# A three-stage decoder layer on one core: reordering the prologue in front of the batch loop

## The chip, the cores and the metric

The kernel runs on one core of a Trainium2 chip. The time is device microseconds (us) of one execution. Five engines work from queues of their own, each strictly in its written order: PE (TensorE), DVE (VectorE), ACT (ScalarE), POOL (GpSimd) and SP (SyncE), which here only issues DMAs. They meet through semaphores.

## The reference

For each of 8 batches of 256 tokens with 512 features:

```
i, f, g = x @ Wi.T, x @ Wf.T, x @ Wg.T
a = sigmoid(f);  b = silu(i) * (1 - a)
h[t] = a[t] * h[t-1] + b[t]                      # scan over tokens
xg = h * silu(g)
y = xg * rsqrt(mean(xg^2) + 1e-5) * w_norm
x1 = layernorm(x + y @ Wo.T)
x2 = layernorm(x1 + wkv(w, u, k=x1, v=ctx))      # exponential weights, a scan over tokens
w1q, w2q = per-row int8 quantise-dequantise of w_gate_up (2816x512), w_down (512x1408)
gate, up = quantised(x2) @ w1q.T
out = layernorm(x2 + quantised(silu(gate) * up) @ w2q.T)
```

## The kernel before, in words

A batch passes through three stages. Stage 1 is `project(b, k)`: six half projections (k = 0, 1 forget, 2, 3 input, 4, 5 gate), each 24 matmuls because every fp32 operand is split into a high and a low part (`split_half`, `split_x`: high part on ACT, low part on DVE or POOL). ACT reads each half (`read_projection`), DVE does `weigh_inputs`, `recurrence`, `gating`, ACT and DVE split the result (`split_states`), PE multiplies it by Wo (`project_out(b, t)`, one of two blocks of 128 tokens) and sums its squares (`sum_squares`), then `mean_square`, `rms_scale`, `residual_1`, `layer_norm_1`, `rstd_1` and `normalise_1` give x1. Stage 2 turns x1 (`turn_keys`), takes exponentials and scans (`sum_weights`, `denominator`, `sum_values`, `numerator`, `divide`, `refine`), turns the result back (`turn_values`) and normalises it (`residual_2`, `layer_norm_2`, `rstd_2`, `normalise_2`, `scale_2`). Stage 3 is the quantised MLP (`turn_inputs`, `mlp_up`, `scale_products`, `silu`, `hidden`, `hidden_max_row`, `mlp_down`). All three run at once on three neighbouring batches in a loop; in front of the loop a prologue fills this pipeline, written out call by call for each engine. The diff touches only the prologue (lines 438 to 476 of SP, 724 to 797 of PE, 1062 to 1150 of ACT, 1374 to 1405 of POOL, 1786 to 1850 of DVE).

The prologue also prepares the MLP weights, in 15 loads q = 0 to 14 ("rows"), of which 0 to 10 hold two blocks of w_gate_up (512 KB) and 11 to 14 one block of w_down (704 KB). A load passes through five engines: `load_rows` (SP), `weigh_rows` (DVE: row maximum, scale, inverse), `round_rows` (POOL), `turn_rows` (PE, 8 or 11 transposes), `keep_rows` (ACT). Loads 0 to 10 share three buffers of the ring, so load q waits until load q - 3 has been turned:

```
elif q >= RING:
    sp.wait_ge(rows_turned, last + 1)
```

`last` is 3 for q = 6, 4 for q = 7 and 5 for q = 8. The scales of the rows also go out to HBM and back: `turn_scales(0)` (PE), `read_scales(0)` (ACT), `store_scales(0)` (SP, waits for the former), `spread_scales(0)`. SP's list has `store_scales(0)` between loads 7 and 8.

`exp_tables` and `silu_tables` switch ACT's function table. `warm_up` and `keep_busy(n)` are transposes of the identity whose output is not used; `keep_busy` stands where PE would have nothing to do.

## Time and profile before

| | |
|---|---|
| median of 3 runs | 418.21 us (418.01 to 418.85) |
| profiled execution | 415.5 us, span of its instructions 413.7 us |
| PE busy | 90% of the span |
| DVE, ACT, POOL busy | 88%, 77%, 54% |
| mean granted TensorE clock | 0.978 |

The median lies 2.7 us above the profiled execution. All durations below are of that one profiled execution, so a sum is made against its span and carried over to the median as a difference.

Up to about 130 us the prologue runs, then the loop, with PE busy nearly all the time, and from about 345 us the last batches. The slices of the page show the prologue as the part with digits below 9 on PE. Work that arrives later at the loop moves all that follows.

### The profile page before, as it was taken

How to read it: one execution, taken by the hardware profiler on the slowest of the kernel's cores; microseconds unless marked ns; L12 is line 12 of the kernel's file. 1: busy time of each engine (PE TensorE's matmuls, PEld its weight loads, DVE VectorE, ACT ScalarE, POOL GpSimd, SP SyncE). 2: the span in 40 equal slices, each digit the busy share in tenths (PEclk: the TensorE clock that was granted, in tenths of full speed). 3: DMA queues.
4: the chain of work that ended last, by engine and by line, in shares of the span. 5: the costliest groups of instructions: out<-in, count | busy, mean ns of one | idle time of the engine just before them, and what ended most of it. 6: DMA issues, size and time to landing. Idle time of an engine off the chain costs nothing.

```text
span 413.7 us, 7886 instructions
## 1 busy us (share of the span) xinstructions
PE 370.7 (90%) x2756; PEld 290.6 (70%) x2778; DVE 362.6 (88%) x620; ACT 320.0 (77%) x422; POOL 223.8 (54%) x274
## 2 busy tenths in 40 slices
PE   7798899989898899999999999999999999386862
PEld 7797798769775778678776977697759774133331
DVE  3889899869767999999998999899989998997684
ACT  3688599597928989599959995999599967975671
POOL 1674564833435726674667546654676454745451
PEclk9999999999999999999999999999999999688997
DMA  7978356011200013000400040005000300000101
GB/s 255 370 259 325 102 194 242 0 52 27 103 1 2 0 58 122 2 26 27 153 1 27 3 177 2 25 0 177 0 25 0 128 0 25 25 1 2 51 27 52
DMA packets 12843, 31.75 MB, mean 77 GB/s; under 512 B 2038, under 2 KB 5132, under 8 KB 12812
## 3 DMA queue, kind: packets, MB, share of 16 engines
q1 hardware_dynamic: 12812, 31.35, 21.7%
q8 instruction: 18, 0.29, 0.3%
q14 instruction: 13, 0.11, 0.1%
HBM read 27.14 MB, written 4.21 MB: 76 GB/s over the span
## 4 chain that ended last, share of the span: by engine, by line
PE 50%; DVE 15%; ACT 13%; issue 10%; POOL 8%; DMA 2%; SPq 1%; POOLq 0%; DVEq 0%; ACTq 0%
PE proj_ps L506 29%; PE slot_ps L611 10%; PE slot_ps L646 5%; POOL ring L1300 2%; DMA ring<-w_gate_up_dram 2%; ACT L1013 2%; DVE hid_top L1654 2%; PE proj_ps L691 1%; DVE stats L1590 1%; PE slot_ps L631 1%; ACT xqT L955 1%; DVE num L1583 1%; DVE ring L1635 1%; ACT L1017 1%; ACT turn_ps L918 1%
## 5 line engine op out<-in xcount | busy, mean ns | idle before, releaser
L611 PE MATMUL slot_ps<-w1q,xqT 128*128 128x512 bf16 (+1 forms) x377 | 80.1, 362 | 5.7 <-ACT xqT L955 2.9
L1300 POOL TENSOR_TENSOR ring<-ring 128x512 f32<-128x512 f32 (+1 forms) x48 | 61.3, 1284 | 36.0 <-ACT ring L964 36.0
L611 PEld LDWEIGHTS slot_ps<-w1q,xqT 128*128 128x128 bf16 x384 | 35.9, 98 | 44.8 <-issue 3.5
L506 PE MATMUL proj_ps<-x_high,proj_high 128*128 128x256 f32 x384 | 64.8, 290 | 0.8 <-ACT proj_high L891 0.4
L506 PE MATMUL proj_ps<-x_low,proj_high 128*128 128x256 f32 x384 | 61.5, 282 | 0.0
L506 PE MATMUL proj_ps<-x_high,proj_low 128*128 128x256 f32 x384 | 61.5, 282 | 0.0
L506 PEld LDWEIGHTS proj_ps<-x_high,proj_high 128*128 128x128 f32 x384 | 53.1, 189 | 2.8 <-issue 0.7
L506 PEld LDWEIGHTS proj_ps<-x_high,proj_low 128*128 128x128 f32 x384 | 52.7, 188 | 0.0
L506 PEld LDWEIGHTS proj_ps<-x_low,proj_high 128*128 128x128 f32 x384 | 52.6, 188 | 0.0
L1275 POOL TENSOR_TENSOR den<-den,q_state 128x512 f32<-128x512 f32 x16 | 27.5, 1736 | 38.0 <-ACT q_state L924 38.0
L646 PE MATMUL slot_ps<-w2q,hqT 128*128 128x512 bf16 x161 | 42.1, 405 | 6.6 <-ACT hqT L978 5.8
L964 ACT ACTIVATE ring<-ring,zero_bias,x_scale 128x512 f32<-128x512 f32 (+1 forms) x48 | 36.8, 771 | 10.4 <-DVE ring L1635 10.3
L971 ACT ACTIVATE ring<-ring,round_bias,hid_inv 128x768 f32<-128x768 f32 (+1 forms) x32 | 29.6, 966 | 10.4 <-DVE hid_inv L1676 10.4
L1635 DVE TENSOR_TENSOR ring<-slot_ps,scale_rows 128x512 f32<-128x512 f32 (+1 forms) x48 | 30.6, 638 | 6.8 <-PE slot_ps L611 6.4
L646 PEld LDWEIGHTS slot_ps<-w2q,hqT 128*128 128x128 bf16 x176 | 16.6, 103 | 25.9 <-issue 8.9
L1236 POOL TENSOR_SCALAR ring<-ring,row_inv 128x512 f32<-128x512 f32 (+1 forms) x24 | 25.3, 1068 | 17.4 <-DVE row_inv L1730 17.4
L1552 DVE TENSOR_TENSOR_SCAN p_state<-decay_col,num 128x256 f32<-128x256 f32 x32 | 31.7, 1049 | 0.0
L1638 DVE TENSOR_TENSOR ring<-slot_ps,scale_rows 128x512 f32<-128x512 f32 (+1 forms) x48 | 30.5, 636 | 0.0
L1654 DVE TENSOR_REDUCE hid_top<-ring 128x1 f32<-128x1408 f32 x15 | 24.1, 1609 | 4.5 <-POOL ring L1300 4.5
L1270 POOL TENSOR_TENSOR num<-num,c_sb 128x512 f32<-128x512 f32 x16 | 20.5, 1286 | 13.7 <-ACT num L908 13.4
L978 ACT ACTIVATE hqT<-slot_ps,half_bias 128x768 bf16<-128x768 f16 (+1 forms) x32 | 25.3, 836 | 3.2 <-PE slot_ps L631 3.1
L1017 ACT ACT_TABLE_LOAD x18 | 23.1, 1283 | 1.0 <-PEq L1986 0.7
(146 smaller groups left out, 809.8 us busy)
## 6 DMA issues: line engine op xcount, KB each, us to landing
ring<-w_gate_up_dram SPq DMA_DIRECT2D x11, 512.0 KB, 4.3
forget<-xT_dram SPq DMA_DIRECT2D x8, 512.0 KB, 3.6
x_sb<-x_dram SPq DMA_DIRECT2D x8, 512.0 KB, 3.6
c_sb<-cT_dram SPq DMA_DIRECT2D x8, 512.0 KB, 4.4
out_dram<-late SPq DMA_DIRECT2D x16, 256.0 KB, 2.1
late<-w_down_dram SPq DMA_DIRECT2D x2, 704.0 KB, 6.6
ring<-w_down_dram SPq DMA_DIRECT2D x2, 704.0 KB, 4.2
scale_rows<-scratch_dram SPq DMA_DIRECT2D x2, 704.0 KB, 5.9
```

The costliest lines, as they stand in the source:

```text
L506: last = nc.tensor.matmul(out, a, b, start=(i == 0), stop=(i == len(terms) - 1))
L611: last = nc.tensor.matmul(slot_ps[:, s, half * 512:half * 512 + width], xqT[:, par, d, t * P:(t + 1) * P], w1q[:, d, half * I + at:half * ...
L646: last = nc.tensor.matmul(slot_ps[:, s, 0:D], hqT[:, i, :], w2q[:, i, :], start=(i == 0), stop=(i == IB - 1))
L964: nc.scalar.activation(g, g, ACT.Silu, bias=zero_bias[:, :], scale=x2_scale[:, par, t:t + 1]).then_inc(silu_ready, 1)
L971: nc.scalar.activation(h, h, ACT.Identity, bias=round_bias[:, :], scale=hid_inv[:, t:t + 1]).then_inc(hid_rounded, 1)
L1017: nc.scalar.preload_act_table_set("silu_and_others")
L1275: nc.gpsimd.tensor_tensor(blocks(den, h), blocks(den, h), blocks(rec_copy, h), ALU.mult).then_inc(newton_ready, 1)
L1300: nc.gpsimd.tensor_tensor(hid, hid, gate_buf[:, at:at + width], ALU.mult).then_inc(hid_ready, 1)
L1552: last = nc.vector.tensor_tensor_scan(p_state[:, c, 1:], decay_col[:, c:c + 1].to_broadcast([P, T]), num[:, c, :], 0.0, ALU.mult, ALU.add)
L1635: nc.vector.tensor_tensor(gate_buf[:, at:at + width], slot_ps[:, s, 0:width], scale_rows[:, at:at + width], ALU.mult).then_inc(gate_scaled, 1)
L1638: nc.vector.tensor_tensor(hid_buf(t)[:, at:at + width], slot_ps[:, s, 512:512 + width], scale_rows[:, I + at:I + at + width], ALU.mult).th ...
L1654: nc.vector.tensor_reduce(hid_top[:, :], hid_buf(t)[:, 0:I], AX.X, ALU.max, apply_absolute_value=True).then_inc(hid_top_ready, 1)
```

## The change

SP issues the halves of the projection weights ahead of the rows. PE does three projections before the first `turn_rows`, each of the others before one; `turn_rows(3)` stands in front of `project_out(0, 0)`, and 4 and 5, the scales, 6 and 7 stand together behind `project_out(0, 1)`. DVE's `gating(0)` and `biases` come earlier among the `weigh_rows`, `weigh_rows(7)` comes after `layer_norm_1(0)`, and `residual_2(0)`, `layer_norm_2(0)` come ahead of `weigh_rows(12)`, `normalise_2` and `scale_2` ahead of `weigh_rows(13)`. ACT and POOL follow. PE's filler transposes shrink: 80 to 64 at the start, 56 to 28 before `project_out(0, 0)`, 92 to 32 before `turn_values(1, 0)`.

```diff
@@ SP
             load_half((0, 0))
             load_xT(0)
-            load_rows(0)
             load_half((0, 1))
             load_columns()
             load_half((1, 0))
+            load_rows(0)
+            load_half((1, 1))
+            load_half((2, 0))
             load_rows(1)
-            load_half((1, 1))
+            load_half((2, 1))
             load_rows(2)
-            load_half((2, 0))
-            load_half((2, 1))
+            load_half((OUT_PROJ, 0))
+            load_half((OUT_PROJ, 1))
             load_rows(3)
             load_x(0)
             load_rows(4)
-            load_half((OUT_PROJ, 0))
             load_rows(5)
-            load_half((OUT_PROJ, 1))
             load_rows(11)
@@ PE
-                for _ in range(40):
+                for _ in range(32):
...
             project(0, 0)
+            project(0, 1)
+            project(0, 2)
             turn_rows(0)
-            project(0, 1)
+            project(0, 3)
             turn_rows(1)
-            project(0, 2)
+            project(0, 4)
             turn_rows(2)
-            project(0, 3)
-            project(0, 4)
             project(0, 5)
-            for q in range(3, 6):
-                turn_rows(q)
-            turn_scales(0)
             keep_busy(28)
-            pe.wait_ge(xg_ready, 1)
-            keep_busy(28)
+            turn_rows(3)
             project_out(0, 0)
             sum_squares(0)
             project_out(0, 1)
+            turn_rows(4)
+            turn_rows(5)
+            turn_scales(0)
             turn_rows(6)
             turn_rows(7)
             keep_busy(16)
...
             project_out(1, 0)
             sum_squares(1)
+            project_out(1, 1)
             turn_rows(12)
-            project_out(1, 1)
...
             project(2, 5)
-            pe.wait_ge(proj_read, 2 * PROJ + 5)
-            keep_busy(28, proj_ps[:, 0, 0:P // 2])
-            pe.wait_ge(num_ready, 4)
-            keep_busy(36, proj_ps[:, 0, 0:P // 2])
-            pe.wait_ge(h_ready, 3)
-            keep_busy(28, proj_ps[:, 0, 0:P // 2])
+            pe.wait_ge(mlp_read, 3)
+            keep_busy(32)
             turn_values(1, 0)
@@ ACT
             read_projection(0, 1)
+            split_half((2, 1))
+            forget_gate(0)
+            read_projection(0, 2)
+            split_half((OUT_PROJ, 0))
             keep_rows(0)
-            forget_gate(0)
-            split_half((2, 1))
+            split_half((OUT_PROJ, 1))
+            read_projection(0, 3)
             keep_rows(1)
-            read_projection(0, 2)
-            read_projection(0, 3)
-            split_half((OUT_PROJ, 0))
+            read_projection(0, 4)
             keep_rows(2)
-            split_half((OUT_PROJ, 1))
-            read_projection(0, 4)
             read_projection(0, 5)
-            keep_rows(3)
-            read_scales(0)
             split_states(0)
             square(0)
             split_x(1)
+            keep_rows(3)
             keep_rows(4)
             exp_tables()
             decay()
-            for q in range(5, 7):
-                keep_rows(q)
+            keep_rows(5)
+            read_scales(0)
+            keep_rows(6)
...
-            keep_rows(12)
             round_2(0, 0, 0)
             round_2(0, 0, 1)
+            keep_rows(12)
@@ POOL
-            for q in range(6):
+            for q in range(4):
                 round_rows(q)
             pair_squares(0)
+            round_rows(4)
             split_x(1)
+            round_rows(5)
+            rms_scale(0)
             round_rows(6)
-            rms_scale(0)
             round_rows(7)
             rstd_1(0)
...
+            pair_squares(1)
+            rstd_2(0)
+            split_x(2)
             round_rows(12)
-            pair_squares(1)
-            split_x(2)
-            rstd_2(0)
@@ DVE
             split_first_x()
+            split_half((0, 1))
+            split_half((1, 0))
             weigh_rows(0)
-            split_half((0, 1))
+            split_half((1, 1))
+            split_half((2, 0))
             weigh_rows(1)
-            split_half((1, 0))
-            split_half((1, 1))
+            split_half((2, 1))
             weigh_rows(2)
-            split_half((2, 0))
+            split_half((OUT_PROJ, 0))
+            weigh_inputs(0)
+            recurrence(0)
+            split_half((OUT_PROJ, 1))
+            biases()
             weigh_rows(3)
-            split_half((2, 1))
+            gating(0)
             weigh_rows(4)
-            weigh_inputs(0)
+            split_states(0)
             weigh_rows(5)
-            recurrence(0)
-            split_half((OUT_PROJ, 0))
-            gating(0)
-            split_half((OUT_PROJ, 1))
-            split_states(0)
-            biases()
-            for q in range(6, 8):
-                weigh_rows(q)
             mean_square(0)
+            weigh_rows(6)
             residual_1(0, 0)
             residual_1(0, 1)
             layer_norm_1(0)
+            weigh_rows(7)
             weigh_rows(8)
...
             gating(1)
-            weigh_rows(12)
-            split_states(1)
             residual_2(0, 0)
             residual_2(0, 1)
+            split_states(1)
             layer_norm_2(0)
+            weigh_rows(12)
+            normalise_2(0, 0)
+            mean_square(1)
+            scale_2(0, 0)
             weigh_rows(13)
-            mean_square(1)
-            normalise_2(0, 0)
             residual_1(1, 0)
-            scale_2(0, 0)
             residual_1(1, 1)
```

On PE from the end of `project(0, 5)` to the start of `project(1, 0)`, before (L506 with proj_high is `project`, with wo_high `project_out`; L665 is `turn_rows`, L678 `turn_scales`, L691 `keep_busy`, L540 `sum_squares`):

```order
L506 MATMUL proj_ps<-x_low,proj_high 128x256 x4
L665 MATMUL slot_ps<-identity,ring 128x128 x24
L678 MATMUL slot_ps<-identity,row_scale 11x128
L691 MATMUL slot_ps<-identity 128x128 x56
L506 MATMUL proj_ps<-wo_high,xg_high 128x512 x4
...
L506 MATMUL proj_ps<-wo_low,xg_high 128x512 x4
L665 MATMUL slot_ps<-identity,ring 128x128 x16
L691 MATMUL slot_ps<-identity 128x128 x16
L506 MATMUL proj_ps<-x_high,proj_high 128x256 x4
```

and the same stretch now:

```order
L691 MATMUL slot_ps<-identity 128x128 x28
L665 MATMUL slot_ps<-identity,ring 128x128 x8
L506 MATMUL proj_ps<-wo_high,xg_high 128x512 x4
...
L506 MATMUL proj_ps<-wo_low,xg_high 128x512 x4
L665 MATMUL slot_ps<-identity,ring 128x128 x16
L678 MATMUL slot_ps<-identity,row_scale 11x128
L665 MATMUL slot_ps<-identity,ring 128x128 x16
L691 MATMUL slot_ps<-identity 128x128 x16
L506 MATMUL proj_ps<-x_high,proj_high 128x256 x4
```

Transposes of rows 4 and 5 moved from ahead of the two `project_out` to behind them.

On DVE from `mean_square(0)` (msq) over `residual_1` and `layer_norm_1` (stats, mv) to the next rows, before:

```order
L1724 TENSOR_REDUCE row_max<-ring 128x2
L1727 TENSOR_SCALAR row_scale<-row_max 128x2
L1730 RECIPROCAL row_inv<-row_scale 128x2
L1504 TENSOR_SCALAR msq<-turn_ps 128x2
L1512 SCALAR_TENSOR_TENSOR inp<-proj_ps,rms,x_sb 128x512 x2
L1520 BN_STATS stats<-inp 128x6 x2
L1524 BN_AGGR mv<-stats 128x2 x2
L1724 TENSOR_REDUCE row_max<-ring 128x2
```

and now (three lines lower in number for the same functions):

```order
L1501 TENSOR_SCALAR msq<-turn_ps 128x2
L1721 TENSOR_REDUCE row_max<-ring 128x2
L1724 TENSOR_SCALAR row_scale<-row_max 128x2
L1727 RECIPROCAL row_inv<-row_scale 128x2
L1509 SCALAR_TENSOR_TENSOR inp<-proj_ps,rms,x_sb 128x512 x2
L1517 BN_STATS stats<-inp 128x6 x2
L1521 BN_AGGR mv<-stats 128x2 x2
L1721 TENSOR_REDUCE row_max<-ring 128x2
```

Before, the row maxima ahead of msq were of loads 6 and 7 and the one behind mv of load 8; now load 6 stands behind msq, and the one behind mv is of load 7.

On POOL in front of the first norm's `rstd_1(0)` (ve, neg_mean), now; L1231 is `round_rows`, two instructions to a load, L1244 `rms_scale(0)`:

```order
L1231 TENSOR_SCALAR ring<-ring,row_inv 128x512 x2
L1244 TENSOR_TENSOR rms<-msq,minus_half 128x2
L1231 TENSOR_SCALAR ring<-ring,row_inv 128x512 x4
L1250 TENSOR_TENSOR ve<-mv,eps_col 128x2
```

Loads 6 and 7 are both rounded between `rms_scale(0)` and `rstd_1(0)`; before, load 6 came ahead of `rms_scale(0)`.

## Rows read from the trace of the kernel before

**Rows 1.** The page: span, engines, and the granted clock in 40 slices.

```profile
span 413.7 us, 7886 instructions
PE 370.7 (90%) x2756; PEld 290.6 (70%) x2778; DVE 362.6 (88%) x620; ACT 320.0 (77%) x422; POOL 223.8 (54%) x274
PEclk9999999999999999999999999999999999688997
```

**Rows 2.** Timeline, PE, 36 to 47 us: start, us, line, tile, count [idle before].

```profile
36.89 1.16 PE L506 MATMUL proj_ps<-wo_high,xg_high 128*128 128x512 f32 x4 [0.48 <-DVE xg_low L1498]
43.47 0.62 PE L665 MATMUL slot_ps<-identity,ring 128*128 128x128 f16 x8
46.97 0.71 PE L506 MATMUL proj_ps<-x_high,proj_high 128*128 128x256 f32 x4
```

**Rows 3.** Timeline, DVE, 25 to 70 us, the same columns.

```profile
25.70 1.31 DVE L1479 SCALAR_TENSOR_TENSOR inp<-forget,inp 128x1024 f32<-128x1024 f32 x1 [0.55 <-ACT inp L859]
26.93 1.21 DVE L1724 TENSOR_REDUCE row_max<-ring 128x2 f32<-128x1024 f32 x1
28.60 2.29 DVE L1487 TENSOR_TENSOR_SCAN inp<-forget,inp 128x1024 f32<-128x1024 f32 x1
35.42 1.21 DVE L1498 TENSOR_TENSOR xg_low<-inp,xg_high 128x1024 fp32r<-128x1024 f32 x1
36.55 1.25 DVE L1735 TENSOR_SCALAR u_cap<-u_col 128x4 f32<-128x4 f32 x1
37.91 2.25 DVE L1740 TENSOR_SCALAR key_bias<-key_bias 128x4 f32<-128x4 f32 x1
51.91 1.60 DVE L1724 TENSOR_REDUCE row_max<-late 128x1 f32<-128x1408 f32 x1
53.84 1.26 DVE L1534 TENSOR_TENSOR_SCAN q_state<-decay_col,turn_ps 128x256 f32<-128x256 f32 x2
69.36 0.69 DVE L1577 SCALAR_TENSOR_TENSOR num<-den,turn_ps 128x510 f32<-128x510 f32 x1 [0.46 <-POOL den L1275]
```

**Rows 4.** Timeline, POOL's `split_x(1)`, and ACT's `keep_rows(6)` and `silu_tables`.

```profile
37.74 2.39 POOL L1226 TENSOR_TENSOR x_low<-forget,x_high 128x1024 fp32r<-128x1024 f32 x1
...
44.13 1.12 ACT L992 ACTIVATE w1q<-slot_ps,half_bias 128x1024 bf16<-128x1024 f16 x1 [2.39 <-PE slot_ps L665]
45.26 1.28 ACT L1017 ACT_TABLE_LOAD   x1
```

**Rows 5.** DMA issues at 34.1, 34.5 and 35.6 us: median us to landing last.

```profile
ring<-w_gate_up_dram SPq DMA_DIRECT2D x1, 512.0 KB, 4.1
c_sb<-cT_dram SPq DMA_DIRECT2D x1, 512.0 KB, 4.9
late<-w_down_dram SPq DMA_DIRECT2D x1, 704.0 KB, 5.6
```

**Rows 6.** Windows at the end: us, busy us per engine (instructions), clock, DMA.

```profile
355.00:360.00 5.00, 1.44 (x11) 1.01 (x11) 4.96 (x9) 5.00 (x7) 4.04 (x4) 0.50 0.12 47
```

**Rows 7.** Timeline, PE: the first row at this gap, then the same matmuls twice.

```profile
357.27 0.82 PE L631 MATMUL slot_ps<-identity,ring 128*128 128x128 f16 x6 [4.66 <-ACT ring L971]
360.64 4.47 PE L646 MATMUL slot_ps<-w2q,hqT 128*128 128x512 bf16 x10 [0.54 <-ACT hqT L978]
...
151.65 2.32 PE L646 MATMUL slot_ps<-w2q,hqT 128*128 128x512 bf16 x10
```

**Rows 8.** Timeline, PE, the start of `project(2, 0)`.

```profile
81.89 0.71 PE L506 MATMUL proj_ps<-x_high,proj_high 128*128 128x256 f32 x4 [0.25 <-DVE inp L1512]
```

**Rows 9.** Timeline, PE, DVE and POOL, 110 to 119 us, around the 92 fillers.

```profile
110.04 5.31 PE L691 MATMUL proj_ps<-identity 128*128 128x128 f16 x92 [1.96 <-ACT gate L859]
116.27 1.28 DVE L1583 TENSOR_TENSOR num<-x,turn_ps 128x512 f32<-128x512 f32 x2 [4.38 <-PE turn_ps L575]
118.61 1.61 DVE L1654 TENSOR_REDUCE hid_top<-ring 128x1 f32<-128x1408 f32 x1
113.75 1.01 POOL L1300 TENSOR_TENSOR ring<-ring 128x384 f32<-128x384 f32 x1 [0.72 <-ACT ring L964]
```

## The prediction

> **What bounds the kernel now.** The page comes first: PE is busy for 90% of the span at nearly the full clock [rows 1]. It bounds the loop, and there the change touches nothing. The prologue is another matter, so I read the timeline of each engine up to 130 us and ask at each meeting point who came last.
>
> At the first output projection that is DVE. PE waited, through fillers, until xg_low was written at 36.6 and began at 36.89 [rows 2, 3]. The second half of that output projection ended at 43.5, where `turn_rows(6)` follows, and `project(1, 0)` started at 46.97 [rows 2]. From 53.84 to 71 us DVE is the chain: the scans of batch 0 begin directly behind `weigh_rows(11)` and only one wait of 0.46 us on POOL interrupts them [rows 3]. At 110 us PE itself is late: its 92 fillers run to 115.35 [rows 9] while DVE, done with `gating(2)`, waits 4.38 us for `turn_values(1)`.
>
> **Part 1: projections earlier.** The weights now come first in SP's list, and PE no longer waits for rows between the projections. Five more projections of 2.9 us from 11.4 us on, with the waits for ACT's readings, end near 28 us, 2.5 earlier. It buys little, since DVE is late, not PE. My count for DVE: `weigh_inputs` waits for the reading of the fourth half, which ACT reaches only after splitting both halves of Wo, at about 24.95 (before 25.70, [rows 3]). Behind it stand, start to start, 1.23 (`weigh_inputs`, 25.70 to 26.93), 2.3 (scan), 1.33 (second Wo half), `biases`, 1.57 (load 3, 26.93 to the scan's memset at 28.50), 1.14 (`gating`), 1.57 (load 4), 1.13 (`split_states`) [rows 3]. `biases` are three instructions on 4 columns and took from 36.55 to 40.07; the long one ended at 40.16, within 0.03 us of POOL's `split_x(1)` at 40.13 [rows 3, 4]. In the change POOL has nothing to do at that moment, so I take 0.5 us. Sum: xg_low at 35.9 instead of 36.6, so `project_out(0, 0)` starts at 35.95, 0.9 us ahead of 36.89 [rows 2]. If they cost 3.5 again, it is 38.9.
>
> The Trainium skill, "SBUF — State Buffer", section on the two separate sides, says that DVE and GpSimd share a port pair under an exclusive lock held for the whole instruction. By that the trace agrees, and the sum takes the 0.5.
>
> **Part 2: fillers removed in front of `project_out(0, 0)`.** After P(0,5) PE now has 28 fillers (1.6 us), to 29.5. Then it waits for load 3: DVE weighs it behind `biases`, POOL rounds it, and `turn_rows(3)` runs at about 33.5 for 0.45 us; then nothing until 35.9. That is 6 of 6.5 us idle. At the end of the kernel 4.66 us of idle were followed by a granted clock of 0.50, the 1.2 GHz level, over 355 to 360 us [rows 6, 7], and the ten matmuls behind the gap took 4.47 us against 2.32 at full clock: 2.15 us more. I take that for the output projection. The bounds are 0 and 3 us (all 6.7 us of the two halves at half rate would be more, but the clock came back within the row behind). So the second half ends at 35.95 + 6.75 + 2.15 = 44.8, where it was 43.5.
>
> The Trainium skill, "TensorE: Matmul & The Clock Gate", Part 1, states that the throttled clock is the default and that only activity releases it. It speaks against this cut of fillers; by it the drop is certain here (423.3), where without it the total would be 421.2.
>
> **Part 3: one burst of transposes.** This decides. The ring has three buffers, so load 7 cannot be issued before `turn_rows(4)`, nor load 8 before `turn_rows(5)`, and both now stand behind `project_out(0, 1)`. Before, they were turned near 32 us and loads 6 to 8 were in flight by 34 [rows 5]. Now: `turn_rows(4)` ends at 45.25. Load 7 lands 3.8 us later (rows of 512 KB take 4.1 to land, [rows 5]), at 49.1; 1.6 us DVE, 1.4 POOL: load 7 is turned at 52.6, and `rstd_1(0)`, behind it on POOL, starts at 52.2 instead of 47.4. ACT keeps load 4 from 45.25 (1.1), switches tables (1.28), does `decay` (0.5), keeps load 5 (1.05), reads the scales (0.3) [rows 4]: 49.5. Only then does SP store them and issue load 8, at 49.9. Landings: load 8 at 53.9 and, spaced as the landings 38.2, 39.4 and 41.2 [rows 5], c at 55.2, load 12 at 57.0, load 9 at 58.3, load 10 at 59.6. DVE, in strict order: load 9 until 59.9, load 10 until 61.5, load 11 until 63.4 (1.93 for a load of w_down, 51.91 to 53.84, [rows 3]). The scans of batch 0 start at 63.4 instead of 53.84: 9.55 late, and the wait of 0.46 on POOL goes, so 9.1 us late at `gating(1)`. ACT and PE cannot hide it. Their own chain (load 7 turned, 16 fillers, `project(1, 0)`, reading it behind `normalise_1`) is about as late: `project(1, 0)` starts near 53.5 to 54.4 against 46.97, the more so as PE idled from 46 to 52 and its clock may be down again.
>
> **Part 4: second norm ahead of two row maxima.** Normalising and scaling come about 3.8 us earlier on DVE, since `rstd_2` no longer waits behind the rounding of load 12 and `split_x(2)`. But `turn_inputs(0)` stands behind `project(2, 0)` on PE, which started on DVE's `residual_1(1, 0)` [rows 8], and that residual keeps its place: behind load 12, load 13 and the norm. I get `normalise_1(1)` 0.2 us earlier. Gain 0.2; bounds 0 and 1.4, the lead of `layer_norm_1(1)`.
>
> **Part 5: 92 fillers to 32.** They now start right behind `project(2, 5)` and take 1.8 us, ending before `refine(1, 1)`. `turn_values(1)` starts at 110.5 instead of 115.2. Not all of it is gained: `hidden_max_row(0, 0)`, at 118.61, needs POOL's last product, which ended at 113.75 + 1.01 = 114.76 [rows 9]. Gain 118.6 - 114.8 = 3.8 us. PE had 1.96 us of idle here before without a fall in its clock; that stays about the same.
>
> The 16 start fillers less (0.3 us) lie ahead of part 1, whose end DVE sets: nothing.
>
> **Sum.** +9.1 - 0.2 - 3.8 = +5.1 us on the span of 413.7, so 418.8. The median of runs stands 2.7 us above the profiled execution, and the difference carries over: 418.21 + 5.1 = 423.3. A change of less than about 0.2% (0.8 us) cannot be told from none here.
>
> **Rivals.**
> - The clock does not fall at the output projection (the short `turn_rows(3)` in the gap holds it): 2.1 us less, 421.2. For it: 1.96 us of idle at 108 us did nothing. Against: the gap is three times that.
> - More is lost: `biases` meet POOL again (3.1 us) or a second fall of the clock makes ACT's chain the later one (1 to 3 us): 425.5 to 427.
> - Faster: the loads do not bind. If load 7 were issued before `project_out(0, 1)` ends, by 41 us, it would land before `layer_norm_1(0)` is over, and the lead of 0.9 us would live on: 418.21 - 0.9 - 0.2 - 3.8 = 413.3. It would need SP's wait to be satisfied by an earlier turn, and the order of PE says no.
> - No change: the late loads cost just what the fillers give back, about 4 us, if the transfers of loads 9 and 10, alone in the queue, land 5 us earlier than I space them: 418.2.
>
> **Chances.** Forecast 0.45 (its own range 422 to 425), no fall of the clock 0.20, more lost 0.20, no change 0.05, faster 0.10. So faster 0.10, same 0.05, slower 0.85. The range that leaves out the last two cases goes from 419.8 to 427.0.
>
> **What would show it.** Right: in the new profile SP issues load 7 behind `turn_rows(4)`, at 45 us; DVE sits idle for 2 to 4 us before row maxima, released by DMA; the first q_state scan starts near 63 us; the clock of a window in 33 to 40 us is 0.5; the PE filler before `turn_values(1)` counts 32 and the DVE wait for turn_ps is under 1 us. Wrong: the first scan starts before 58 us, or the loop begins earlier than before.

## The result: 2.2% slower, and the profile after

| | before | changed |
|---|---|---|
| median of 4 runs | 418.26 us (418.01 to 418.85) | 426.44 us (426.24 to 427.26) |
| ratio, 95% interval | 1 | 1.0216 (1.0185 to 1.0247) |
| span of the profiled execution | 413.7 us | 424.5 us |
| mean granted TensorE clock | 0.978 | 0.961 |

The forecast was slower, 423.3 us, with 427.0 as the upper end. The median lies inside that range and the ratio just above the 1.0210 that 427.0 is to 418.21: the direction is right, the size is 3 us short. The ratio is that of the runs as recorded; the two medians of the table alone give 1.0196, which its interval takes in, so that the change is slower beyond doubt, and whether by 2% is not. The page of the changed kernel:

```profile
span 424.5 us, 7700 instructions
...
PE 374.4 (88%) x2674; PEld 291.7 (69%) x2674; DVE 360.9 (85%) x620; ACT 319.7 (75%) x422; POOL 221.4 (52%) x274
...
PEclk9996889898999999999999999999999999889988
```

[rows 1] have 0.6 at the worst of the clock, and only at the end. Here it is below 9 in five slices of the first quarter too. PE is busy 3.7 us longer although it runs fewer instructions. The timelines of PE and SP show the places (start, us, line, tile, count, idle before):

```profile
34.66 1.04 PE L665 MATMUL slot_ps<-identity,ring 128*128 128x128 f16 x8 [4.57 <-POOL ring L1231]
36.28 2.05 PE L506 MATMUL proj_ps<-wo_high,xg_high 128*128 128x512 f32 x4 [0.59 <-DVE xg_low L1495]
...
41.68 1.17 PE L506 MATMUL proj_ps<-wo_high,xg_high 128*128 128x512 f32 x4
...
44.57 1.07 PE L665 MATMUL slot_ps<-identity,ring 128*128 128x128 f16 x16
...
51.69 1.03 PE L665 MATMUL slot_ps<-identity,ring 128*128 128x128 f16 x8 [4.59 <-POOL ring L1231]
...
54.19 1.20 PE L506 MATMUL proj_ps<-x_high,proj_high 128*128 128x256 f32 x4
...
94.54 1.08 PE L506 MATMUL proj_ps<-x_high,proj_high 128*128 128x256 f32 x4 [2.27 <-DVE inp L1509]
...
121.77 1.96 PE L691 MATMUL slot_ps<-identity 128*128 128x128 f16 x32
124.34 1.09 PE L575 MATMUL turn_ps<-identity,num 128*128 128x128 f32 x8 [0.60 <-DVE num L1574]
```

```profile
35.73 9.82 SPq L396 DMA_DIRECT2D ring<-w_gate_up_dram  x2
...
49.84 0.36 SPq L396 DMA_DIRECT2D ring<-w_gate_up_dram  x1
```

`project_out(0, 0)` starts at 36.28, 0.6 us ahead of [rows 2], but its first four matmuls take 2.05 us instead of 1.16. The burst starts at 44.57. Load 7, the second of the two issues from 35.73 on, goes out when `turn_rows(4)` has ended, near 45.5; load 8 at 49.84. `project(1, 0)` starts at 54.19 (46.97 in [rows 2]) and `project(2, 0)` at 94.54 (81.89 in [rows 8]), with four matmuls in 1.20 and 1.08 us instead of 0.71. The windows of the same kernel (busy us of PE, PEld, DVE, ACT, POOL, then clock, DMA share, GB/s) give the clock:

```profile
36.00:40.00 4.00, 3.72 (x9) 3.01 (x10) 1.49 (x4) 1.64 (x2) 4.00 (x4) 0.50 0.42 131
52.00:56.00 4.00, 4.00 (x31) 4.00 (x30) 1.55 (x3) 1.52 (x2) 1.22 (x3) 0.50 1.01 395
96.00:100.00 4.00, 4.00 (x37) 3.95 (x36) 2.31 (x6) 0.81 (x2) 2.61 (x5) 0.74 0.47 132
```

Twice the lower level of 1.2 GHz (0.50), and once a mix. In the second the DMA engines are full as well (1.01): loads 8, 9, c and 12 are all behind the burst now. What DVE saw, and behind it POOL's rows of the second norm and ACT's `normalise_1(1)`:

```profile
30.54 0.17 DVE L1737 TENSOR_SCALAR key_bias<-key_bias 128x4 f32<-128x4 f32 x1
...
48.56 1.22 DVE L1721 TENSOR_REDUCE row_max<-ring 128x2 f32<-128x1024 f32 x1 [1.49 <-DMA ring<-w_gate_up_dram]
...
53.86 1.22 DVE L1721 TENSOR_REDUCE row_max<-ring 128x2 f32<-128x1024 f32 x1 [3.68 <-DMA ring<-w_gate_up_dram]
...
59.30 1.22 DVE L1721 TENSOR_REDUCE row_max<-ring 128x2 f32<-128x1024 f32 x1 [3.83 <-DMA ring<-w_gate_up_dram]
...
62.08 0.78 DVE L1724 TENSOR_SCALAR row_scale<-row_max 128x2 f32<-128x2 f32 x1
...
64.91 1.26 DVE L1531 TENSOR_TENSOR_SCAN q_state<-decay_col,turn_ps 128x256 f32<-128x256 f32 x2
...
79.60 1.21 DVE L1490 TENSOR_TENSOR inp<-inp,gate 128x1024 f32<-128x1024 f32 x1
...
84.75 1.59 DVE L1721 TENSOR_REDUCE row_max<-late 128x1 f32<-128x1408 f32 x1
...
86.64 3.49 DVE L1599 TENSOR_SCALAR x_even<-num,mv,rstd 128x512 f32<-128x512 f32 x2
...
90.16 1.22 DVE L1606 TENSOR_REDUCE x_max<-x_even 128x2 f32<-128x1024 f32 x1
...
93.64 1.41 DVE L1509 SCALAR_TENSOR_TENSOR inp<-proj_ps,rms,x_sb 128x512 f32<-128x512 f32 x2
...
129.08 1.62 DVE L1651 TENSOR_REDUCE hid_top<-ring 128x1 f32<-128x1408 f32 x1 [0.90 <-POOL ring L1295]
```

```profile
85.84 2.40 POOL L1221 TENSOR_TENSOR x_low<-forget,x_high 128x1024 fp32r<-128x1024 f32 x1
88.22 1.62 POOL L1231 TENSOR_SCALAR late<-late,row_inv 128x1408 f32<-128x1408 f32 x1
```

```profile
100.77 1.51 ACT L931 ACTIVATE x<-inp,shift,rstd 128x512 f32<-128x512 f32 x2
```

DVE waits for the landings of loads 7, 8 and 9 (1.5, 3.7 and 3.8 us), and the first scan comes at 64.91 instead of 53.84. `normalise_2`, 86.64, takes 3.49 us for two instructions, while POOL does `split_x(2)` until 88.24 and rounds load 12 until 89.84.

Four of these starts cut every kernel's span into legs: the first scan of batch 0 (first q_state), `gating(1)`, `normalise_1(1)` on ACT, and the first `hidden_max_row`. The table has them for all kernels run, in us, each as the distance of starts in the kernel's own timeline. The names are those of the experiments below.

| kernel | to first scan | to gating(1) | to normalise_1(1) | to hidden_max_row | to the end | span |
|---|---|---|---|---|---|---|
| before | 53.84 | 16.12 | 16.96 | 31.69 | 295.1 | 413.7 |
| changed | 64.91 | 14.69 | 21.17 | 28.31 | 295.4 | 424.5 |
| b_filler | 54.57 | 15.72 | 16.96 | 28.31 | 293.7 | 409.3 |
| b_norm2 | 54.34 | 15.71 | 21.17 | 31.67 | 295.0 | 417.9 |
| b_front | 65.60 | 14.69 | 17.09 | 31.68 | 294.8 | 423.9 |
| a_busy | 61.35 | 15.72 | 21.06 | 28.30 | 296.8 | 423.2 |
| a_burst | 61.61 | 16.17 | 21.06 | 28.30 | 296.9 | 424.0 |
| b_lock | 54.89 | 15.86 | 18.33 | 33.31 | 294.9 | 417.3 |
| a_norm2 | 66.18 | 14.69 | 18.33 | 28.30 | 295.5 | 423.0 |
| b_bias | 53.18 | 15.91 | 16.97 | 28.32 | 295.5 | 409.9 |
| b_free | 53.61 | 16.03 | 18.99 | 28.32 | 293.9 | 410.8 |
| a_all | 60.46 | 14.69 | 16.95 | 28.30 | 293.8 | 414.2 |

From before to changed: +11.07 - 1.43 + 4.21 - 3.38 + 0.33 = +10.8, the difference of the spans. The medians differ by 8.2, since the profiled execution of before (415.5 us) was one of its shorter ones.

### The profile page after: what moved, and what is told of

It is laid out like the page before. It is cut to its first block, busy times and chain, and to the rows that moved or that the text cites. A ratio compares the mean times of both kernels' runs of the same rounds, so it can differ in the third digit from the quotient of the medians.

```text
span 424.5 us, 7700 instructions
## 1 busy us (share of the span) xinstructions
PE 374.4 (88%) x2674; PEld 291.7 (69%) x2674; DVE 360.9 (85%) x620; ACT 319.7 (75%) x422; POOL 221.4 (52%) x274
## 3 DMA queue, kind: packets, MB, share of 16 engines
HBM read 27.14 MB, written 4.21 MB: 74 GB/s over the span
## 4 chain that ended last, share of the span: by engine, by line
PE 48%; DVE 20%; issue 11%; ACT 10%; DMA 4%; POOL 4%; SPq 2%; POOLq 0%; DVEq 0%; ACTq 0%
PE proj_ps L506 28%; PE slot_ps L611 12%; PE slot_ps L646 3%; DMA late<-wgT_dram 2%; DVE row_max L1721 2%; POOL ring L1295 2%; DMA ring<-w_gate_up_dram 2%; ACT xqT L950 2%; DVE stats L1587 2%; DVE p_state L1549 1%; PE turn_ps L564 1%; PE slot_ps L631 1%; DVE ring L1632 1%; DVE hid_top L1651 1%; DVE q_state L1531 1%
## 5 line engine op out<-in xcount | busy, mean ns | idle before, releaser
L611 PE MATMUL slot_ps<-w1q,xqT 128*128 128x512 bf16 (+1 forms) x384 | 81.5, 362 | 6.0 <-ACT xqT L950 2.7
L506 PE MATMUL proj_ps<-x_high,proj_high 128*128 128x256 f32 x384 | 66.1, 295 | 4.1 <-DVE inp L1509 2.3
L506 PE MATMUL proj_ps<-x_high,proj_low 128*128 128x256 f32 x384 | 62.4, 285 | 0.0
L506 PE MATMUL proj_ps<-x_low,proj_high 128*128 128x256 f32 x384 | 62.4, 285 | 0.0
L506 PEld LDWEIGHTS proj_ps<-x_high,proj_high 128*128 128x128 f32 x384 | 54.4, 193 | 5.9 <-issue 4.2
L506 PEld LDWEIGHTS proj_ps<-x_high,proj_low 128*128 128x128 f32 x384 | 53.7, 192 | 0.0
L506 PEld LDWEIGHTS proj_ps<-x_low,proj_high 128*128 128x128 f32 x384 | 53.4, 191 | 0.0
L646 PE MATMUL slot_ps<-w2q,hqT 128*128 128x512 bf16 x176 | 45.3, 404 | 4.7 <-ACT hqT L973 3.7
L959 ACT ACTIVATE ring<-ring,zero_bias,x_scale 128x512 f32<-128x512 f32 (+1 forms) x48 | 36.8, 772 | 10.3 <-DVE ring L1632 10.1
L1231 POOL TENSOR_SCALAR ring<-ring,row_inv 128x512 f32<-128x512 f32 (+1 forms) x24 | 22.6, 956 | 34.3 <-DVE row_inv L1727 34.3
L1549 DVE TENSOR_TENSOR_SCAN p_state<-decay_col,num 128x256 f32<-128x256 f32 x32 | 30.0, 997 | 0.0
L1721 DVE TENSOR_REDUCE row_max<-ring 128x2 f32<-128x1024 f32 (+1 forms) x13 | 16.5, 1270 | 9.0 <-DMA ring<-w_gate_up_dram 9.0
```

What stands on the lines that cost most here:

```text
L506: last = nc.tensor.matmul(out, a, b, start=(i == 0), stop=(i == len(terms) - 1))
L611: last = nc.tensor.matmul(slot_ps[:, s, half * 512:half * 512 + width], xqT[:, par, d, t * P:(t + 1) * P], w1q[:, d, half * I + at:half * ...
L646: last = nc.tensor.matmul(slot_ps[:, s, 0:D], hqT[:, i, :], w2q[:, i, :], start=(i == 0), stop=(i == IB - 1))
L959: nc.scalar.activation(g, g, ACT.Silu, bias=zero_bias[:, :], scale=x2_scale[:, par, t:t + 1]).then_inc(silu_ready, 1)
L1549: last = nc.vector.tensor_tensor_scan(p_state[:, c, 1:], decay_col[:, c:c + 1].to_broadcast([P, T]), num[:, c, :], 0.0, ALU.mult, ALU.add)
```

## The experiments

**The three parts, each alone on the kernel before.** b_filler has only the cut of fillers ahead of `turn_values(1, 0)`, b_norm2 only what concerns the second norm, b_front only the rest. The three together are the change. Of each run the text gives the median, then its ratio to runs of the kernel before made beside it, with the 95% interval, then the span of the profiled execution.

```diff
@@ b_filler: PE
             project(2, 5)
-            pe.wait_ge(proj_read, 2 * PROJ + 5)
-            keep_busy(28, proj_ps[:, 0, 0:P // 2])
...
+            pe.wait_ge(mlp_read, 3)
+            keep_busy(32)
             turn_values(1, 0)
@@ b_norm2: DVE (PE, ACT and POOL as in the change)
             gating(1)
-            weigh_rows(12)
-            split_states(1)
             residual_2(0, 0)
             residual_2(0, 1)
+            split_states(1)
             layer_norm_2(0)
-            weigh_rows(13)
-            mean_square(1)
+            weigh_rows(12)
             normalise_2(0, 0)
-            residual_1(1, 0)
+            mean_square(1)
             scale_2(0, 0)
+            weigh_rows(13)
+            residual_1(1, 0)
             residual_1(1, 1)
```

> The kernel before with one part of the change: the 92 fillers in front of turn_values(1, 0) become 32, behind project(2, 5). Theory (my part 5): turn_values(1, 0) starts near 110.5 us instead of 115.19, hid_top near 115 instead of 118.61, and the whole kernel is 3.4 to 3.8 us shorter. Rival: the fillers held up the clock for what follows, so that the granted clock falls behind 110 us and less than 2 us is won.

Measured: 411.45 us, 0.9873 (0.9828 to 0.9918), span 409.3.

```profile
108.26 1.96 PE L691 MATMUL slot_ps<-identity 128*128 128x128 f16 x32
110.83 1.09 PE L575 MATMUL turn_ps<-identity,num 128*128 128x128 f32 x8 [0.61 <-DVE num L1573]
```

The 32 fillers end before the values are ready, PE waits 0.61 us for DVE, and the fourth leg is 3.38 us shorter. It is 28.3 in every kernel that has this cut and runs the fillers at full clock. This part is a gain of its own. The span is 4.4 us shorter, not 3.4 to 3.8, because the last leg is 1.4 us shorter too, which nothing in the edit explains.

> The kernel before with only the second norm's part (residual_2 and layer_norm_2 ahead of load 12, normalise_2 and scale_2 ahead of load 13, POOL's rstd_2 ahead of split_x(2) and of load 12, project_out(1, 1) ahead of turn_rows(12)). Theory formed from the trace of the changed kernel: the two instructions of normalise_2 take about 3.5 us instead of 1.0, because POOL works on split_x(2) beside them, and project(2, 0) starts 1.5 to 2.5 us later with a fallen clock: 3 to 4.5 us slower than before. Rival (my prediction's part 4): 0.2 us faster, the loss in the changed kernel being one of its late start.

Measured: 422.88 us, 1.0146 (1.01 to 1.0192), span 417.9. The third leg is 21.17 us, to the hundredth that of the changed kernel, against 16.96.

```profile
77.10 3.47 DVE L1602 TENSOR_SCALAR x_even<-num,mv,rstd 128x512 f32<-128x512 f32 x2
```

```profile
84.98 0.72 PE L506 MATMUL proj_ps<-x_high,proj_high 128*128 128x256 f32 x4 [3.76 <-DVE inp L1512]
...
86.02 1.03 PE L506 MATMUL proj_ps<-x_low,proj_high 128*128 128x256 f32 x4
```

The front is that of before, so neither the burst nor a clock that was low earlier has a part in it. The first matmuls behind the 3.76 us of idle run at full speed (0.72 for four), those from 86.02 at the lower (1.03): the fall comes about 1 us after PE is back at work.

> The kernel before with only the front part (the loads, the projections, gating and biases, the burst of transposes, 56 fillers to 28, 160 start fillers' cut) and neither the second norm's nor the late fillers' part. Theory: the scans of batch 0 start near 64.9 us and gating(1) near 79.6, 9.6 us late, and this stays to the end: 9 to 10 us slower than before. Rival: later stages have slack that takes some of it up, under 7 us.

Measured: 425.66 us, 1.0207 (1.0158 to 1.0257), span 423.9. First scan 65.60, `gating(1)` 80.29, 10.3 us late, and it stays so. With the other parts: +10.3 + 4.2 - 3.4 = +11.1 at `hidden_max_row`, for +10.5 measured. The parts add up to within 0.6 us. The span is 10.2 us longer, the median 8.4 above that of before in the same session (417.28), for the 9 to 10 expected.

**Fillers against the clock fall.** a_busy is the changed kernel with PE kept at work ahead of `project_out(0, 0)`.

```diff
-            keep_busy(28)
+            keep_busy(100)
             turn_rows(3)
+            keep_busy(16)
             project_out(0, 0)
```

> The changed kernel with 100 fillers instead of 28 in front of turn_rows(3) and 16 behind it. Theory (clock): the granted clock stays at 1.00 over 32 to 40 us, the twelve matmuls of project_out(0, 0) take 3.0 us instead of 4.75, and what hangs on turn_rows(4) comes 1.5 to 1.7 us earlier, so the kernel is 1.5 us faster than the changed one. Rival: the time of project_out(0, 0) does not lie on the path (its end only opens a wait for the loads that is there anyway), under 0.5 us.

Measured: 425.33 us, 1.0185 (1.013 to 1.024), span 423.2.

```profile
36.02 1.17 PE L506 MATMUL proj_ps<-wo_high,xg_high 128*128 128x512 f32 x4
...
39.71 1.18 PE L506 MATMUL proj_ps<-wo_high,xg_high 128*128 128x512 f32 x4
```

The lower clock is gone there: the first half takes 3.69 us start to start of the second (36.02 to 39.71), where the changed kernel takes 5.40 (36.28 to 41.68). So the fall cost 1.71 there. In b_front and a_norm2, which have the same front as the changed kernel, the same distance is 5.73 and 6.03, a cost of 2.04 and 2.34, and their first scans come 0.7 and 1.3 later. The first scan gained 3.56, `gating(1)` 2.53, more than the fall itself; the span gained only 1.3, since the last leg is 1.4 longer, where the clock falls at other points of the kernel's end than in the changed kernel. `project(1, 0)`, at 52.53, still runs at the lower clock (1.20 us for four matmuls, behind 4.89 us of idle before `turn_rows(7)`). The 1.5 us expected is about what the span shows; why the first scan gained twice the fall was not asked.

**The burst dissolved.** a_burst is the changed kernel with the transposes of loads 4 and 5 spread, POOL's rounding of both pulled ahead to match.

```diff
@@ PE
             project_out(0, 0)
+            turn_rows(4)
             sum_squares(0)
-            project_out(0, 1)
-            turn_rows(4)
             turn_rows(5)
             turn_scales(0)
+            project_out(0, 1)
```

> The changed kernel with the burst of transposes taken apart: turn_rows(4) behind project_out(0, 0), turn_rows(5) and turn_scales(0) behind sum_squares(0), and POOL rounding loads 4 and 5 before pair_squares(0) and split_x(1). The fallen clock at project_out(0, 0) stays. Theory (part 3): SP issues load 7 near 41 us instead of 45.2 and load 8 near 45 instead of 49.8, the scans of batch 0 start 4 to 5 us earlier than the 64.9 of the changed kernel, and the kernel is 4 to 5 us faster than the changed one. Rival: the late start of project(1, 0) holds the chain (ACT's reading of it, exp_tables, the exponentials), and less than 2 us is won.

Measured: 425.37 us, 1.0184 (1.0141 to 1.0226), span 424.0.

```profile
50.84 1.03 PE L665 MATMUL slot_ps<-identity,ring 128*128 128x128 f16 x8 [4.86 <-POOL ring L1231]
...
53.34 1.20 PE L506 MATMUL proj_ps<-x_high,proj_high 128*128 128x256 f32 x4
```

```profile
47.73 1.19 DVE L1721 TENSOR_REDUCE row_max<-ring 128x2 f32<-128x1024 f32 x1
...
61.61 1.26 DVE L1531 TENSOR_TENSOR_SCAN q_state<-decay_col,turn_ps 128x256 f32<-128x256 f32 x2 [1.04 <-ACT turn_ps L907]
```

Loads 7 and 8 go out 4 us earlier, and load 7 is there when DVE comes to it at 47.73. But DVE comes to it only behind `layer_norm_1(0)`, so `turn_rows(7)` runs at 50.84 and `project(1, 0)` at 53.34, 0.85 us earlier and still at the lower clock, behind `turn_rows(7)` and its 4.86 us of idle. The first scan then waits 1.04 us for ACT and gains 3.3, `gating(1)` 1.8, and the time 1.1: the theory's 4 to 5 us did not come, the rival's less than 2 did. The late loads are thus a cause, but not the only one: the order of DVE and ACT in the front holds it a step behind.

**DVE beside POOL.** b_lock is b_norm2 with one more wait: POOL starts `split_x(2)` when both tiles are normalised.

```diff
             rstd_2(0)
+            pool.wait_ge(x2_ready, 2)
             split_x(2)
```

> The kernel before with the second norm's part, and one wait more: POOL starts split_x(2) only when normalise_2 has written both tiles. If POOL's work beside it is what stretches normalise_2, its two instructions take 1.0 us instead of 3.47 and project(2, 0) starts about 1.3 us earlier than the 84.98 of the second norm's part alone (POOL's own chain to rms_scale(1) is the later one now), so the kernel is 1 to 1.5 us faster than that one. Rival: normalise_2 is slow for another reason (a changed operand, PE's or ACT's work): its instructions stay at 3.5 us and the kernel is slower still by the delay of split_x(2).

Measured: 419.63 us, 1.0055 (1.0028 to 1.0082), span 417.3. DVE, POOL and PE:

```profile
77.79 1.00 DVE L1603 TENSOR_SCALAR x_even<-num,mv,rstd 128x512 f32<-128x512 f32 x2
...
78.82 1.22 DVE L1610 TENSOR_REDUCE x_max<-x_even 128x2 f32<-128x1024 f32 x1
80.08 1.22 DVE L1615 TENSOR_SCALAR x_scale<-x_max 128x2 f32<-128x2 f32 x1
```

```profile
78.87 2.41 POOL L1226 TENSOR_TENSOR x_low<-forget,x_high 128x1024 fp32r<-128x1024 f32 x1 [1.84 <-DVE x_even L1603]
```

```profile
112.19 6.94 PE L691 MATMUL proj_ps<-identity 128*128 128x128 f16 x92 [1.96 <-ACT gate L859]
```

`normalise_2` takes 1.00 instead of 3.47. The next victim shows the same lock more plainly: `scale_2`'s small instruction at 80.08, two elements per partition, takes 1.22 us instead of 0.17 and ends at 81.30, within 0.02 us of POOL's end (78.87 + 2.41). The reduction at 78.82, which runs beside the same POOL instruction, keeps its 1.22. The third leg falls to 18.33, with the clock at full. Of what is left over before, 1.37 us, the lock on that small instruction is 1.05 (1.22 less 0.17); in the new order it lies ahead of `residual_1(1, 0)`. The rest is the order itself. The median is 3.25 us under that of b_norm2, but those are other sessions, and the span is only 0.6 shorter, since part was lost again: behind 1.96 us of idle the 92 fillers ran at the lower clock (6.94 us; 5.31 in [rows 9] behind the same idle), which is the 1.6 us of the fourth leg.

a_norm2 makes the same edit in the changed kernel, with fillers in PE's gap.

```diff
@@ POOL
             rstd_2(0)
+            pool.wait_ge(x2_ready, 2)
             split_x(2)
@@ PE
             project_out(1, 1)
+            keep_busy(32)
             turn_rows(12)
```

> The changed kernel with two edits around the second norm: POOL waits until both tiles of x(1) are normalised before it starts split_x(2), and 32 filler matmuls stand between project_out(1,1) and turn_rows(12). Theory (the second norm lost 4.2 us, 2.5 of them because normalise_2 on DVE was held beside POOL's split_x(2), 1.7 because project(2,0) then ran at the lower clock level): normalise_2 takes 1.0 us instead of 3.49, project(2,0) starts near 93.2 instead of 94.54, its 24 matmuls take about 2.95 us instead of 4.63, the hidden layer's first tile comes 2.5 to 3.5 us earlier than 129.08, the run is at 423 to 424. Rival (the low clock there has another reason than PE's idle time in front of project(2,0), such as the two earlier gaps): the matmuls still take over 4 us and the hidden layer comes only 1.3 us earlier, 425.

Measured: 424.84 us, 1.0176 (1.0131 to 1.022), span 423.0.

```profile
87.92 1.00 DVE L1601 TENSOR_SCALAR x_even<-num,mv,rstd 128x512 f32<-128x512 f32 x2
...
93.58 1.41 DVE L1511 SCALAR_TENSOR_TENSOR inp<-proj_ps,rms,x_sb 128x512 f32<-128x512 f32 x2
```

```profile
94.47 0.71 PE L506 MATMUL proj_ps<-x_high,proj_high 128*128 128x256 f32 x4 [0.66 <-DVE inp L1511]
```

The third leg is 18.33 us, 2.84 shorter, as the theory has it; `hidden_max_row` is only 1.6 earlier, because this run's first scan was 1.27 later, with the longer clock fall at `project_out(0, 0)` told above. The time alone (424.84) lies by the rival's 425. The leg decides between them, and it is the leg of b_lock. `scale_2`'s small instruction was held here too, 1.22 us at 90.21.

**Biases first.** b_bias is b_filler with `biases()` moved ahead of `weigh_inputs(0)`; there POOL is idle up to 25.61, when it begins to round load 4.

```diff
             weigh_rows(4)
+            biases()
             weigh_inputs(0)
...
             split_states(0)
-            biases()
```

> The kernel before with 92 fillers cut to 32, and biases() moved ahead of weigh_inputs(0), where DVE waited 0.55 us and POOL rounds load 4. If POOL's pair_squares and split_x(1) are what made its three small instructions take 3.5 us, they take 0.3 to 1.5 us there, mean_square(0) comes up to 2.5 us earlier, and layer_norm_1(0) 0.5 to 0.9 us earlier: 0.5 to 0.9 us faster than with the fillers alone. Rival: they meet POOL's rounding there and hold weigh_inputs(0), 0 to 1 us slower.

Measured: 411.53 us, 0.9867 (0.9837 to 0.9897), span 409.9, no different from b_filler.

```profile
25.69 0.65 DVE L1736 TENSOR_SCALAR key_bias<-key_bias 128x4 f32<-128x4 f32 x1
...
38.22 2.37 DVE L1723 TENSOR_SCALAR row_scale<-row_max 128x2 f32<-128x2 f32 x1
```

```profile
38.17 2.40 POOL L1222 TENSOR_TENSOR x_low<-forget,x_high 128x1024 fp32r<-128x1024 f32 x1
```

The three instructions take 0.9 us (25.43 to 26.34) in place of 3.6, the last of them, beside POOL's rounding, 0.65, but `split_x(1)` on POOL (38.17) now holds the next small one, `row_scale`, from 38.22 to 40.59. The lock was moved, not removed. `hidden_max_row` comes 1.2 us earlier than in b_filler, and the last leg is 1.8 longer, so that the time gains nothing.

**Another form of the second norm.** b_free is b_bias with the second norm's part in another order; against that part as it is in the change:

```diff
@@ POOL
             rstd_2(0)
+            rms_scale(1)
             split_x(2)
             round_rows(12)
-            rms_scale(1)
@@ DVE
             scale_2(0, 0)
+            residual_1(1, 0)
             weigh_rows(13)
-            residual_1(1, 0)
@@ PE
             project_out(1, 1)
+            project(2, 0)
             turn_rows(12)
-            project(2, 0)
```

> The same and the second norm's part in another form: POOL does rms_scale(1) between rstd_2(0) and split_x(2) (and so waits for normalise_2 and mean_square(1) first), residual_1(1, 0) stands ahead of load 13, and project(2, 0) ahead of turn_rows(12). Theory: normalise_2 takes 1.0 us, project(2, 0) starts about 0.7 us earlier than in the kernel before and its clock does not fall, so 0.3 to 0.9 us faster than the one with biases moved. Rival: turn_inputs(0), behind one more burst of transposes, comes no earlier: the same within 0.3 us.

Measured: 415.35 us, 0.9937 (0.9906 to 0.9968), span 410.8. The third leg is 18.99, 2.0 longer than in b_bias: 

```profile
78.98 1.92 DVE L1610 TENSOR_SCALAR x_scale<-x_max 128x2 f32<-128x2 f32 x1
```

POOL's `split_x(2)`, 78.49 to 80.87 there, holds `scale_2`, and `residual_1(1, 0)` stands behind it. That is not all: counted from `gating(1)`, `project(2, 0)` starts only 0.36 us later than in b_bias (12.31 for 11.95), and 1.66 of the 2.0 come behind it. `turn_rows(12)` now follows `project(2, 0)` on PE, and ACT, which keeps load 12 at 85.73 before it normalises, comes to `normalise_1(1)` at 88.63, 1.3 us after POOL had its shift ready. Which of the two weighs more was not separated. The theory expected a gain here, the rival the same time, and both were wrong.

**All named causes taken away.** a_all is the changed kernel with the second norm's part undone, the edits of a_busy and a_burst, and two more:

```diff
@@ PE
             turn_rows(6)
+            keep_busy(28)
             turn_rows(7)
@@ DVE
             weigh_rows(6)
+            weigh_rows(7)
             residual_1(0, 0)
             residual_1(0, 1)
             layer_norm_1(0)
-            weigh_rows(7)
```

> The changed kernel with its named losses taken away together, 32 filler matmuls in the loop kept: the second norm's part undone; 100 fillers ahead of turn_rows(3) and 16 behind it; turn_rows(4) behind project_out(0,0), turn_rows(5) behind sum_squares(0), POOL's rounds 4 and 5 earlier, 28 fillers ahead of turn_rows(7), DVE's weigh_rows(7) ahead of residual_1(0,0). Theory (late loads behind the one burst, the lower clock of project_out(0,0) and project(1,0), and the second norm make up the loss, and the front's two parts are not additive since either alone leaves the other to hold the first scan): first q_state scan at 57 to 58.5 instead of 64.91, second norm as before the change, hidden layer's first tile near 118 to 119.5 instead of 129.08, time about 416 to 418. Rival (the loss sits in the queue order of the front as a whole, whatever the burst): first scan stays at 61 or later, time 421 or more.

Measured: 415.72 us, 0.9957 (0.9922 to 0.9992), span 414.2.

```profile
49.63 1.22 DVE L1723 TENSOR_REDUCE row_max<-ring 128x2 f32<-128x1024 f32 x1 [0.65 <-DMA ring<-w_gate_up_dram]
...
55.09 1.22 DVE L1723 TENSOR_REDUCE row_max<-ring 128x2 f32<-128x1024 f32 x1 [3.83 <-DMA ring<-w_gate_up_dram]
...
60.46 1.26 DVE L1533 TENSOR_TENSOR_SCAN q_state<-decay_col,turn_ps 128x256 f32<-128x256 f32 x2
```

10.3 us of span are won back of the 10.8, but with the fillers' gain still in it: beside b_filler, which has the same fillers, `hidden_max_row` is 4.8 us later (120.40 for 115.56, and for the 118 to 119.5 expected). The first scan misses its range by 2 us: load 9 still lands at 55.09, 5.5 us behind load 8 at 49.63, since c and load 12 lie between them in the queue and are issued with them. At `gating(1)` it is still 5.2 us later than before (75.15 for 69.96): part of the delay of the front is neither the burst nor the clock, and what remains of it was not taken apart further. One thing the trace shows is that the ring no longer holds load 8: `turn_rows(5)` was done by 42.1, yet SP issues load 8 at 45.41, right behind `store_scales(0)` at 44.99, which waits for ACT's `read_scales(0)` (44.62 to 44.96). In the kernel before, SP was through with `store_scales(0)` at 34.1. No run moved the scales. Of the 10.3 us won, 4.5 lie there, 4.2 in the third leg and 1.6 in the last, which no edit touches. What the cut of fillers gives, b_filler has without that loss.

b_filler and b_bias, 411.5 us, are the fastest kernels of the study, 1.3% under before and some 3.5% under the changed one.

## Why the prediction came out short

- **Part 1, projections earlier:** right. The biases took 0.16 to 0.17 us each (the last at 30.54), 0.5 in all. `project_out(0, 0)` started at 36.28 for 35.95. The terms listed add up to 35.7, not to the 35.9 that the text took.
- **Part 2, clock fall:** right in kind, and the term of 2.15 lies amid the measured 1.71, 2.04 and 2.34, all of it in the first half. The second half ended at 44.73 for 44.8.
- **Part 3, the burst:** the chain went as written: load 8 issued at 49.84 (49.9), `project(1, 0)` at 54.19 (53.5 to 54.4). Load 9 landed at 59.3 for 58.3, and `row_scale` of load 10 was held to 0.78 us, so the first scan came 11.07 late instead of 9.55. Between it and `gating(1)`, 1.43 went away and not 0.46; the rest is mainly in the four scans of p_state, 2.34 us from 69.09 on for 3.88 from 58.02 on before. The two errors nearly cancel: parts 1 to 3 give 9.64 at `gating(1)` for 9.1. The reason given was too narrow, though: without the burst, a_burst is still 7.8 us late at `gating(1)`, and a_all, without the clock falls too, 5.2.
- **Part 4, second norm: the step that failed.** It was "Gain 0.2; bounds 0 and 1.4" and cost 4.21, in the changed kernel and in b_norm2 alike. The step said that `residual_1(1, 0)` "keeps its place: behind load 12, load 13 and the norm". It does not: before, `scale_2(0, 0)` stands behind it, now ahead. From `gating(1)` to that residual it is 14.04 us (79.60 to 93.64) for 11.04 before: `scale_2` adds 1.54 (from its start at 90.16 to the next row maximum at 91.70), `normalise_2`, held by `split_x(2)` and the rounding behind it, 2.49 (3.49 less 1.00), and a wait of 1.03 for POOL's rstd goes. `project(2, 0)` starts 0.90 behind it in both. From there to `normalise_1(1)` it is 6.23 us, and 4.73 in a_norm2 at full clock: the fall costs 1.5, of which 1.2 against before (5.03). 3.00 + 1.21 = 4.21. The lead that the step counted on was not there either: behind `gating(1)` the norm started 3.1 us earlier (7.04 for 10.13), for the 3.8 forecast, and ended only 0.6 earlier. Both mechanisms stood in other parts of the prediction, the lock in part 1 and the fall in part 2; they weren't asked for here. That the norm came "earlier on DVE" meant that `rstd_2` had been pulled ahead of `split_x(2)`, and that is just what set the norm beside it.
- **Part 5, fillers:** right, 3.38 for 3.8. POOL's product still sets `hidden_max_row`, at 129.08 behind 0.90 us of waiting.

With part 4 at +4.2 and part 5 at -3.4 the sum is +9.9 and 428.1, against 426.44 and a span of +10.8. That 426.44 lies in the span of the rival "more is lost", 425.5 to 427, is luck: the biases did not meet POOL (0.5 us), and the second fall of the clock, which did come (1.20 us at 54.19), did not make ACT's chain the later one, since DVE went from load 11 into the first scan without a wait.

Of the lock, the Trainium skill, "SBUF — State Buffer", section on the two separate sides, says that it holds for a whole instruction. The rows agree for TENSOR_SCALAR: the small ones of 2.37 and 1.22 us end within 0.02 us of POOL's, and the two of `normalise_2` at 90.13, 0.3 behind the 89.84 of POOL's second one, the rounding. The reductions beside the same POOL instructions went on undisturbed.

## What to carry to other kernels

When an instruction is moved, look at what runs on the engine it shares memory with at its new time, not only at what it waits for; a held instruction that is moved away leaves its place to the next one. Cut a kernel's prologue into legs between a few landmarks and compare legs, since a leg in the middle repeats to 0.1 us or so (the third is 16.95 to 17.09 in the five kernels that have its old order), where 13 runs of the kernel before in one session range from 414.7 to 420.3 us. A change of several parts deserves one run for each: here one part alone was worth 1.3% and the others hid it. Each run here that took away one cause only, a_busy and a_burst, won about 1 us of the median.

## What was not expected

- Which DVE instructions POOL holds depends on their kind: TENSOR_SCALAR with 2 to 512 elements per partition was held for up to 2.5 us beside POOL's 128x1024 TENSOR_TENSOR, TENSOR_REDUCE of 1024 or 1408 elements was not (1.22 at 78.82 in b_lock, 1.59 at 84.75 in the changed kernel). A TENSOR_SCALAR with one element per partition was not held either: `row_scale` of load 12 at 86.37 took 0.15 us in the middle of `split_x(2)` (85.84 to 88.24), where two elements took 1.22 at 80.08 in b_lock.
- The clock's fall is not the same for the same gap. Behind 1.96 us of idle, 92 fillers took 5.31 us before and 6.94 in b_lock; behind 3.76 us in b_norm2 the first matmuls still ran at full speed and those from 86.02 on at the lower clock. That is a reason for a range on such a term, not for a number. What decides it was not isolated.
- The last leg, where all kernels run the same program, varied from 293.7 to 296.9 us. In the last six slices of the page, the clock digits of the three shortest (b_filler, b_free, a_all) are 799999 or 789999, those of the two longest (a_busy, a_burst) 688988; the others lie between without such an order. Why was not tried.
